# K transposed by VectorE and DRAM instead of TensorE, v's first batch ahead of K V, in a fused two-layer graph kernel

## The reference

```python
h = relu(layernorm(x))
z_l, z_g, v = h @ W_lang.T, h @ W_grav.T, h @ W_V.T
zn = z_l / max(norm(z_l), EPS)
A_l = max(zn @ zn.T, 0) * not_eye
d2 = max(sq + sq.T - 2 * z_g @ z_g.T, 0)        # sq = sum(z_g * z_g)
A_g = exp(-d2 / (2 * sigma**2)) * not_eye
K = w_l * row_stochastic(A_l * adj) + (1 - w_l) * row_stochastic(A_g * adj)
x = x + (K @ v) @ W_O.T
h = relu(layernorm(x))
x = x + einsum('bnf,nm->bmf', h, adj * adj) + bias
```

## Time and profile before

| | |
|---|---|
| time, median of 3 runs | 1233.65 us (1232.67 to 1234.98) |
| the profiled execution | 1233.85 us, its span 1232.1 us |
| PE busy | 1199.0 us, 97% |
| DVE busy | 1062.1 us, 86% |
| ACT busy | 714.5 us, 58% |
| POOL busy | 610.9 us, 50% |
| 16 DMA engines, mean of queue 1 | 38.4% |
| chain that ended last | PE 93%, DVE 3% |
| granted TensorE clock, mean | 0.992 |

### The profile page before, as it was taken

How to read it: one execution, slowest core, us unless ns; L and a number is a source line. 1 busy time by engine, 2 the same in 40 slices (tenths; PEclk the granted TensorE clock), 3 DMA queues, 4 the chain that set the end, 5 groups by cost and what they waited for, 6 DMA issues and landing times.

```text
span 1232.1 us, 22833 instructions
## 1 busy us (share of the span) xinstructions
PE 1199.0 (97%) x6076; PEld 1023.3 (83%) x6076; DVE 1062.1 (86%) x1892; ACT 714.5 (58%) x1324; POOL 610.9 (50%) x991
## 2 busy tenths in 40 slices
PE   7989999999999999999999999999999999999994
PEld 7777888888888888888888888888888888888882
DVE  5667888899888889888888988888898888899878
ACT  5344655665565566556566655556665555665543
POOL 1203554545655444665454466545456554545545
PEclk9999999999999999999999999999999999999998
DMA  7122234344333444433343443344443334443302
GB/s 267 52 77 77 75 113 136 127 128 145 111 96 118 140 128 132 138 117 95 120 136 128 136 121 118 102 126 133 127 141 113 108 112 135 129 126 111 111 1 103
DMA packets 115457, 145.10 MB, mean 118 GB/s; under 512 B 20848, under 2 KB 52720, under 8 KB 115440
## 3 DMA queue, kind: packets, MB, share of 16 engines
q1 hardware_dynamic: 114864, 144.57, 38.4%
q10 hardware_dynamic: 576, 0.33, 0.1%
HBM read 62.46 MB, written 49.87 MB: 91 GB/s over the span
## 4 chain that ended last, share of the span: by engine, by line
PE 93%; DVE 3%; ACT 1%; SPq 1%; issue 1%; DMA 0%; POOL 0%; DVEq 0%; POOLq 0%
PE ring L944 76%; PE p_ps L998 14%; PE kt_ps L957 1%; PE ring L1042 1%; SPq L247 1%; DMA x_ring<-in_L_gnn_W_lang 0%; ACT h2f L501 0%; DVE bn L663 0%; DVE x_ring L698 0%; ACT h L419 0%; DVE chain L802 0%; PE ring L1051 0%; DVE v_lo L589 0%; DVE x_ring L660 0%; DVE ln L676 0%
## 5 line engine op out<-in xcount | busy, mean ns | idle before, releaser
L342 POOL TENSOR_TENSOR h_lo<-h2f,h_hi 128x512 fp32r<-128x512 f32 x124 | 156.7, 1292 | 323.3 <-ACT h_hi L508 323.1
L944 PE MATMUL ring<-hT_hi,Lw_hi 128*128 128x512 f32 x640 | 250.5, 391 | 7.5 <-DVE hT_lo L609 4.3
L944 PE MATMUL ring<-hT_hi,Lw_lo 128*128 128x512 f32 x640 | 250.4, 391 | 0.0
L944 PE MATMUL ring<-hT_lo,Lw_hi 128*128 128x512 f32 x640 | 250.4, 391 | 0.0
L589 DVE TENSOR_TENSOR y_lo<-ring,y_hi 128x512 fp32r<-128x512 f32 x256 | 169.7, 682 | 46.8 <-ACT y_hi L440 46.5
L944 PE MATMUL ring<-MT_hi,hT_hi 128*128 128x512 f32 x512 | 199.4, 389 | 1.4 <-DVE MT_lo L589 1.4
L944 PE MATMUL ring<-MT_hi,hT_lo 128*128 128x512 f32 x512 | 199.2, 389 | 0.0
L944 PE MATMUL ring<-MT_lo,hT_hi 128*128 128x512 f32 x512 | 199.2, 389 | 0.0
L440 ACT ACTIVATE y_hi<-ring 128x512 fp32r<-128x512 f32 x256 | 152.2, 597 | 79.1 <-PE ring L944 75.1
L477 ACT ACTIVATE v_hi<-ring 128x512 fp32r<-128x512 f32 x128 | 76.0, 594 | 190.1 <-PE ring L944 190.1
L327 POOL TENSOR_TENSOR x_ring<-x_ring,bias_sb 128x512 f32 (+1 forms) x124 | 157.8, 1304 | 1.9 <-ACT h2f L501 1.9
(11 more groups left out here) (163 smaller groups left out, 2536.1 us busy)
## 6 DMA issues: line engine op xcount, KB each, us to landing
x_ring<-in_x SPq DMA_DIRECT2D x32, 1024.0 KB, 5.3
out<-x_ring SPq DMA_DIRECT2D x128, 256.0 KB, 2.6
h_turned<-h SPq DMA_DIRECT2D x496, 64.0 KB, 2.0
p_dram<-chain SPq DMA_DIRECT2D x62, 256.0 KB, 2.5
h<-p_dram SPq DMA_DIRECT2D x248, 64.0 KB, 2.6
rn_cols<-rn_dram SPq DMA_DIRECT2D x31, 256.0 KB, 4.0
x_ring<-in_L_gnn_W_lang SPq DMA_DIRECT2D x4, 256.0 KB, 5.2
h2f<-in_L_gnn_W_grav SPq DMA_DIRECT2D x1, 1024.0 KB, 8.9
```

Source lines behind the costliest of these rows:

```text
L342: pool.tensor_tensor(h2[1][:, b], h2f[:, b], h2[0][:, b].bitcast(F32), ALU.subtract)\
L944: mm = pe.matmul(out, lhsT, rhs, start=(k == 0), stop=(k == len(terms) - 1))
```

## The change

K of all groups but the last is transposed as P is: DVE transposes its blocks (`turn_K`, behind combine), SP stores them to DRAM and fetches them with four transfers, ahead of turn_h; ACT's `kt_copy` and DVE's `kt_lo` read the fetched tile. PE's transposes_K leave the loop. On PE v's first batch stands ahead of K V. On DVE kt_lo moves behind the first diagonal, the squares and v_lo(0) ahead of the additions, and turned_lo(i+1, 0) ahead of the fourth statistics. ACT's kt_copy moves behind the copies of P.

```diff
@@ sync @@
+            def turn_K(g):
+                sp.wait_ge(k_blocks, g + 1)
+                sp.dma_start(k_dram, K_blocks.rearrange("p j b q -> p j (b q)")).then_inc(k_stored, 16)
+                sp.wait_ge(k_stored, 16 * g + 16)
+                for j in range(NQ):
+                    sp.dma_start(K_turned[j * Q:(j + 1) * Q].rearrange("r i b q -> r i (b q)"),
+                                 k_dram[:, j].rearrange("(i r) e -> r i e", r=Q)).then_inc(k_turned, 16)
...
+                if not isinstance(i, int) or i > 0:
+                    turn_K(i - 1)
                 turn_h(i + 1)
                 spread_norms_turn_p(i)
...
@@ scalar @@
                 if before:
-                    kt_copy(i - 1)
                     act.wait_ge(s_ready, 2 * i)
                 for half in range(2):
                     act.wait_ge(p_done, GB * i + 2 * half + 2)
                     act.activation(P_sb[:, 2 * half:2 * half + 2], p_ps[:, 2 * half:2 * half + 2], ACT.Copy)\
                        .then_inc(p_copied, 1)
+                if before:
+                    kt_copy(i - 1)
...
+                    if not lag and b == GB - 1:
+                        turned_hi(i + 1, b)
                     act.wait_ge(v_done, GB * i + b + 1)
-                    act.activation(v[0][:, b], bank(n), ACT.Copy).then_inc(hi_ready, 1)
-                    n += 1
-                    if after:
+                    if before and b == 0:
+                        act.wait_ge(kv_done, GB * (i - 1) + 1)
+                    act.activation(v[0][:, b], bank(n + v_use(b, before)), ACT.Copy).then_inc(hi_ready, 1)
+                    if after and (lag or b < GB - 1):
                         turned_hi(i + 1, b)
...
@@ vector @@
+            def turn_K(g):
+                dve.wait_ge(k_ready, g + 1)
+                dve.wait_ge(p_stored[1], 16 * g + 16)
+                dve.transpose(K_blocks.rearrange("p j b q -> p b j q"),
+                              K[:, :, :].rearrange("p b (j q) -> p b j q", q=Q)).then_inc(k_blocks, 1)
...
                         if before and n == 6:
                             combine(i - 1)
+                            turn_K(i - 1)
...
                 if before:
-                    add(i - 1, 0, n)
-                    add(i - 1, 1, n + 1)
...
-                    diagonal(i, 0)
-                    stats(i - 1, 3)
-                    squares(i, 0)
-                    diagonal(i, 1)
-                    squares(i, 1)
+                    diagonal(i, 0)
+                    kt_lo(i - 1)
+                    squares(i, 0)
+                    diagonal(i, 1)
+                    squares(i, 1)
+                    v_lo(0)
+                    add(i - 1, 0, n + 1)
+                    add(i - 1, 1, n + 2)
+                    dve.wait_ge(drained, use + n + 3)
+                    wait_for(dve, ln2_step, LN_STEPS * (i - 1))
+                    add(i - 1, 2, n + 3)
+                    stats(i - 1, 0)
+                    stats(i - 1, 1)
+                    dve.wait_ge(drained, use + n + 4)
+                    add(i - 1, 3, n + 4)
+                    stats(i - 1, 2)
+                    dve.wait_ge(drained, use + n + 1 + GB)
+                    turned_lo(i + 1, 0)
+                    stats(i - 1, 3)
...
@@ tensor @@
-                    if before and a == 1:
-                        transposes_K(i - 1)
-                if before:
-                    pe.wait_ge(kt_split, i)
-                    for b in range(GB):
-                        k_v(i - 1, b, n + b, use + n + b)
...
+                    mm.then_inc(v_done, 1)
+                    if before and b == 0:
+                        pe.wait_ge(kt_split, i)
+                        for kb in range(GB):
+                            k_v(i - 1, kb, n + 1 + kb, use + n + 1 + kb)
```

End: in the last iteration the squares also move up, v_lo, statistics and combine are put in another order, and layer 1 of group 29 comes behind K V of group 31, into p_ps and kt_ps. Groups 30 and 31 get their bias from PE, by two matmuls more in each product:

```diff
+                if g > NG - 3:
+                    terms = [(spread, bias_parts[0]), (spread, bias_parts[1])] + terms
...
-            for b in range(GB):
-                output_bias(g - 1, b, GB + b)
-            h2_lo(g, 0)
-            for b in range(1, GB):
-                h2_lo(g, b)
-                output(g, b - 1, 2 * GB + b - 1)
-            output(g, GB - 1, 3 * GB - 1)
+            for b in range(GB):
+                late_output(g - 2, b)
+            for b in range(GB):
+                h2_lo(g, b)
+                late_output(g - 1, b)
+            for b in range(GB):
+                late_output(g, b)
```

More of the change, by code:

```diff
@@ L202, in hT_columns, with KT_columns, v_use @@
             return hT[part][:, :, b].rearrange("p c (i q) -> p i c q", q=Q)
+        def KT_columns(part):
+            return KT[part][:, :, :].rearrange("p b (i q) -> p i b q", q=Q)
+        def v_use(b, before):
+            return 0 if before and b == 0 else GB + b
         def x_rows(g, b):
             return x_ring[:, bass.ds(g % SLOTS, 1), b].rearrange("p s d -> p (s d)")
+        LAST_OUTPUTS = [(NG - 2, b) for b in range(GB)] + [(NG - 1, b) for b in range(GB)]
+        LAST_FIRST = PER - GB
+        late = [p_ps[:, 0:2].rearrange("p b l m -> p (b l m)"), p_ps[:, 2:4].rearrange("p b l m -> p (b l m)"),
+                kt_ps[:, :, :].rearrange("p b m -> p (b m)")]
+        bias_parts = [w[:, 0] for w in y_rows]
+        spread = y_rows[0][:, 1, 0:P]
         block = ctx.enter_context(nc.Block())
@@ L362, in iteration @@
                     norm1(i + 2)
-                if before and not after:
+                if not after:
+                    pool.wait_ge(bias_hi, 2)
+                    pool.tensor_tensor(bias_parts[1], bias_sb[:, :], bias_parts[0].bitcast(F32), ALU.subtract)\
+                        .then_inc(bias_split, 1)
                     norm2(i - 1)
@@ L732, in iteration @@
                     turn_blocks(i + 1, 3)
-                    if before:
-                        kt_lo(i - 1)
                     if x_next:
@@ L761, in iteration @@
                         lo(MT[1][:, c], bank(n + c), MT[0][:, c], hi).then_inc(drained, 1)
-                n += GB
                 for b in range(GB):
-                    hi = hi + 1
-                    lo(v[1][:, b], bank(n), v[0][:, b], hi)\
-                        .then_inc(drained, 1 if lag or b < GB - 1 else 1 + GB)
-                    n += 1
-                    turned_lo(i + 1, b)
+                    if not lag and b == GB - 1:
+                        turned_lo(i + 1, b)
+                    if not before or b > 0:
+                        v_lo(b)
+                    if (lag or b < GB - 1) and not (before and b == 0):
+                        turned_lo(i + 1, b)
                     if b < 2:
                         turn_p(i, b)
+                n += 2 * GB
                 if lag:
@@ L871, in factor_lo, with lw_lo @@
                                       ALU.subtract).then_inc(side_split, 1)
-            def lw_lo(l, banks, hi_done, done, last=1):
-                for c in range(C):
+            def lw_lo(l, banks, hi_done, done, last=1, c0=0, c1=C):
+                for c in range(c0, c1):
                     dve.wait_ge(hi_done, c + 1)
@@ L984, in iteration @@
                         n += 1
-                        if not before and n == 1:
-                            pe.wait_ge(side_split, C)
+                        if not before and n == 2:
+                            transposes_w_o(C // 2)
+                            transposes_w_o(C // 2 + 1)
                         if not before and n == BANKS - 1:
@@ L1002, in iteration @@
                             mm.then_inc(p_done, 1)
-                    if before and a == 1:
-                        transposes_K(i - 1)
-                if before:
-                    pe.wait_ge(kt_split, i)
-                    for b in range(GB):
-                        k_v(i - 1, b, n + b, use + n + b)
-                else:
+                if not lag:
+                    n += GB
+                if not before:
                     pe.wait_ge(w_split, 3 * C)
@@ L1015, in iteration @@
                             .then_inc(setup_mm, 1)
[L1016 to L1017 removed]
                 for b in range(GB):
[L1019 to L1022 removed]
+                    m = n + v_use(b, before)
+                    free(use + m)
+                    for c in range(C):
+                        if not before and b == 0:
+                            pe.wait_ge(drained, use + G_USES + GB + c + 1)
+                        terms = passes([w[:, c, b] for w in hT], [w[:, c] for w in MT])
+                        for k, (lhsT, rhs) in enumerate(terms):
+                            mm = pe.matmul(bank(m), lhsT, rhs, start=(c == 0 and k == 0),
+                                           stop=(c == C - 1 and k == len(terms) - 1))
+                    mm.then_inc(v_done, 1)
[3 more added lines that the diff above has]
+                            k_v(i - 1, kb, n + 1 + kb, use + n + 1 + kb)
                     if b == 0 and not after:
@@ L1028, in iteration @@
                         transposes_rn(i)
-                if lag:
```

(6 more changed lines are left out.)

229 lines of the change are left out of this document (126 added, 103 removed).

## The result

The changed kernel takes 1311.41 us (median of 4 runs, 1310.58 to 1313.0), the kernel before 1233.34 beside it: a ratio of 1.0632 (95% interval 1.0614 to 1.0651), 78.1 us slower. Forecast were 1289, 1238 to 1312. The profiled execution has a span of 1309.8, 77.7 more than before.

The account below looks back on a forecast made before the run. PE bound the kernel before; after the change a loop over SP's DRAM trip was to close at about 38.5 us an iteration: 1233.85 + 68.7 - 13 - 0.2 = 1289 us, range 1238 to 1312.

Parts of the forecast that it names:

- PE's own work: TensorE's matmuls in one iteration: 36.13 us less 0.44 for K's transposes leaves 35.69.
- rival 1: No loop closes in time to delay PE, which stays back to back: 1207 us, chance 0.12.
- Loop A: From sum_s over K's DRAM trip, h's transfers, norm2, row_norms and P's fetch to the next sum_s: 38.2 us.
- Loop C: Without the DRAM trip, from y over K V, additions, norm2 and h2_full to the next y: 36.76 us.
- kt_lo reads SBUF instead of PSUM at the same size of 128x512, nothing: DVE's lo part of transposed K: the move from PSUM to SBUF adds no time.
- The 0.6 above hides it: Ahead of K V on PE: 0.6 us of cover would hide a kt_lo longer by 0.1.
- K not late for K V: Turned K's hi and lo parts are ready 21.5 us after y, against K V's start at 22.06.
- rival 3: K arrives late for K V, shown by waits for KT_lo ahead of it: 1330 us, chance 0.08.
- DVE 33.0 us busy, not the bound: DVE's work per iteration: 32.3 us, 33.0 with K's transpose added, so DVE does not bound.
- The clock's fall in every other iteration: PE's clock after y's wait: half the chance upper level throughout (38.2 us), half falling every iteration (38.9).
- The 38.5: Iteration time taken as the middle between 38.2 and 38.9 us, 2.37 above 36.13.
- Front and end: Shorter PE waits before and after the loop: 7 us saved in front, 6 at the end, together -13.

Follow-up runs that it names:

- e4: Changed kernel with POOL's bias behind row_norms, ahead of norm2, ACT's h2_full behind turned_hi(3), DVE's transpose of P's first half, then fourth statistics, ahead of turned_lo(0): 1210.71 us.
- a4: Changed kernel with POOL's bias addition cut to 8 of 512 columns, the rest of the bias left out: 1309.27 us, ratio 1.0625.
- a1: Changed kernel with row_norms(i) put ahead of norm2(i-1) on POOL: 1287.93 us, ratio 1.0441.
- a2: Changed kernel with ACT's h2_full(0) moved behind turned_hi(3), where the other three stand: 1310.88 us, ratio 1.0635.
- b1: Changed kernel with POOL's bias additions moved behind row_norms(i) and ahead of norm2(i-1): 1282.36 us, ratio 1.0407.

## Why the prediction was right, and where not

The sign was right, and so was the outline: loops of one iteration close later than PE's own work, y waits for hT_lo, and the time before was PE's own. The path that set the time was another than the forecast's.

- **PE's own work, 35.69.** Right: e4 runs at 35.70. It is what the change offers, and what rival 1 (1207) would have made of it.
- **Loop A over SP, 38.2.** Its path failed at one link: turned_lo(0) does not wait for turned_hi(0), DVE comes there 0.2 later by its own row of work. The trip itself was well sized, +24.43 by the forecast and +24.45 measured up to turned_hi(0), partly by luck: K's store is issued 0.4 late (+9.01 behind 624.22, for 8.61), and its landing is 2.03 instead of 2.5. Behind it norm2 and row_norms are 0.2 late (+26.63 and +30.22), and from the norms' issue to P's second fetch it is 3.78 instead of 3.19. Together 38.89, 0.7 more. Only in a4, with a faster DVE, does the forecast's loop A close, at about 39. That norm2 and P's fetch are in the loop that counts is shown by a1, which takes norm2 out and gains 23.5.
- **Loop C over PE, 36.76.** A term of it was mis-sized. By itself it is seen in a1, 38.33, 1.6 more. In the changed kernel it is the shorter one (a2 cuts it for 0.5 us), but the late term lies in both. Three of its four links fit there (5.95 for 6.00, 3.81 for 3.65, 2.76 for 2.93); from y to the first addition it is 26.37 for 24.18, in a1 25.82. The failed sentence is "kt_lo reads SBUF instead of PSUM at the same size of 128x512, nothing". It takes 1.71 us for 0.69; with the second diagonal (1.17 for 0.70) and sqc (0.41 for 0.17) that is 1.7 of the 2.2. In a1, where KT_lo takes 1.60 in the rows, it is the whole 1.6. In the old order K's lo part read PSUM, and the squares stood behind K's additions; in the new one all of them are ahead of the first addition and beside POOL's bias. "The 0.6 above hides it" was true for 0.1, not for 1.0.
- **K not late for K V.** Right for the transfer, wrong for PE: ACT's KT_hi at 638.70 does not wait for DMA, yet PE waits 1.0 us an iteration for KT_lo. The sign that was to show rival 3 is there with another cause.
- **DVE 33.0 us busy, not the bound.** This is the step that hid the path. A sum over an iteration does not see that from sum_s to the fourth statistics (624.22 to 650.04) DVE waits for 0.33 us only. That row, with the added transpose of K (0.71) and the longer KT_lo in it, closed the loop over SP, and every tenth added there lengthens it.
- **The clock's fall in every other iteration.** Not in the steady loop of the changed kernel: its y waits of 1.2 us leave the granted clock at 1.00. In the loop it is 0.72 only behind the third iteration's y, which waits 2.92 (107 to 113 us), and that distance is the 42.1. a4, with waits of 1.1 to 2.6, has the fall behind some of them. The 38.5 was thus a mean of 38.2 and 38.9 for the wrong reason; the loop itself was 0.7 longer. 29 x (39.23 - 38.5) = 21, less 2 for the kernel before (36.19 an iteration, not 36.13), is what the loop's 88.2 has over the 68.7.
- **Front and end.** The front gave 6.9 for 7, the end 3.5 for 6. No run took these apart.

In sum: +68.7 became +88.2, and -13 became -10.4.

## What to carry to other kernels

When an operand moves from PSUM to SBUF, ask what GpSimd does in that very stretch: a lo part of 0.7 us became one of 1.7, and a helper of 4 columns one of 1.05. Before a stage is moved, write down every loop of one iteration with its links, those through an engine's own unbroken order too, and look afterwards which link really waits; here three closed within 1 us of each other, so that single edits gave 0 to 29 us and all that e4 has together 101 (1311.4 to 1210.7). A change that costs 6% can hold the faster kernel: K through DRAM is worth its 12 us, once the statistics, the bias and h2_full stand where they don't close a loop.

## What the runs showed of the hardware that was not expected

VectorE and GpSimd hold each other up, by kinds of operation. Beside GpSimd's 128x512 additions, VectorE's difference of two SBUF tensors took 1711 ns instead of 687, and its scalar operation on 4 columns 1050 instead of 152; a 128x512 addition of GpSimd took 1622 instead of 1293. Transposes (0.69), statistics (0.68) and differences that read PSUM (0.68 to 0.69) were not held. It goes the other way too: norm2's first instruction took 0.58 us for 0.21 beside turned_lo(0). A lo part that lasts 1.0 us longer, less than one of GpSimd's additions, would fit a wait for the end of a running instruction; no row shows that wait by itself. The Trainium skill (SBUF — State Buffer, Who interferes with whom) has a rule for it: a VectorE instruction with two SBUF inputs takes part of a port pair that it shares with GpSimd, against GpSimd instructions that read SBUF, and the later of the two waits for the other's end. The traces agree for the differences (KT_lo, and turned_lo(0) in b1), and the prediction could have had KT_lo's missing 1.0 us from that rule and POOL's rows.

Waits of 1.2 us ahead of y left the granted clock at 1.00; behind one of 2.64 us in a4 (540.16) it was 0.72 over 6 us, matmuls coming every 0.43 us instead of 0.23, with 3.5 us of them at the lower level. The length of the wait alone does not decide it: behind another of 2.64 us in a4 (501.01) it stayed at 1.00, and in b1, where y waits 1.85 us in every iteration, it was 0.72 behind five of these waits, six iterations apart each time, and 1.00 behind others (187 to 193 us). What decides is not shown.
